# Attention on one core: small transfers of the row sums moved to the sync engine, with later steps for the reciprocal, the output and the stack loads

## The chip, the cores and the metric

The kernel runs on one core of one Trainium2 chip. The metric is device time in microseconds (us). Engines are named as in the profile: PE is TensorE (PEld its weight loads), DVE is VectorE, ACT is ScalarE, POOL is GpSimd, SP is the sync engine, which here only issues DMAs. "SPq" and "ACTq" in a row mean the sequencer of that engine, issuing a DMA.

## What is computed

A transformer block with modulation by a condition vector, in float32, for 4 sequences of 1024 tokens, width 512, 16 heads of 32:

```python
ada = jax.nn.silu(c) @ Wada.T + bada
shift_msa, scale_msa, gate_msa, shift_mlp, scale_mlp, gate_mlp = jnp.split(ada, 6, axis=-1)
h = modulate(rmsnorm(x, g1, D), scale_msa, shift_msa)
qkv = h @ Wqkv.T + bqkv          # reshaped to q, k, v of 16 heads
q = rmsnorm(q, gq, hd) * hd ** (-0.5)
k = rmsnorm(k, gk, hd)
attn = jax.nn.softmax(jnp.einsum('bhqd,bhkd->bhqk', q, k), axis=-1)
o = jnp.einsum('bhqk,bhkd->bhqd', attn, v)
...
x = x + gate_msa[:, None, :] * (o @ Wproj.T + bproj)
h = modulate(rmsnorm(x, g2, D), scale_mlp, shift_mlp)
x = x + gate_mlp[:, None, :] * (gelu(h @ Wfc1.T + bfc1) @ Wfc2.T + bfc2)
```

## The kernel before, in words

Three parts follow each other: a setup, attention (`build_attention`), and the projection with the MLP (`build_mlp`). The change lies in attention alone.

Attention is a sequence of 256 **steps** L. A step takes one tile of 128 keys against one chunk of 512 queries, for four heads at once. Eight steps (`NT`) make a **half**: all keys against one query chunk; this document numbers the steps in a half 0 to 7. Two halves make a **group** of four heads (`STEPS` = 16), four groups a sequence (`BSTEPS` = 64). Each half has a number `hh`, 0 to 31.

In a step TensorE multiplies scores (`qk`, line 431) in two pairs of heads, each into its own PSUM tile; ACT takes their exponential into one of three probability buffers (`exponentials`, line 591; `RING` = 3); one step later TensorE multiplies the probabilities with the values (`weigh`, line 444), and VectorE adds them up over the half (`add`, line 677: seven additions of 2.3 us per half). Exponentials wait until the buffer's old contents were both weighed and added. Scores of a step wait for the exponentials of the step before.

Between these, a plan made of tables fills TensorE's time with the projections for later groups. `FILL` gives 4 or 6 products of `unit_products` (line 496) or `v_products` (line 509) to a step. A finished "unit" (one 128 x 512 block of keys or queries of a group) goes through `raw_out` (708), `square` (572), `sum_squares` (468), `logarithm` (562), `inverse_root` (566) and `make_parts` (757 to 765, step table `FIN_AT`). SP stores its two parts to DRAM (`store_parts`, 359, 512 KB) and loads them back in stacked form (`load_stack`, 381, four DMAs of 256 KB per unit). The table `STACK_LOAD` says at which step SP does so: for keys of a group at the earliest in steps 1 (first half of the keys) and 2 of the group before; for queries of half 0 in step 1 of the second half of the group before, for queries of half 1 in step 1 of the group itself. Keys of half 1 are needed at step 4 of the group, queries at the start of their half.

At the end of a half its row sums are inverted. For half `hh`, in steps counted from the start of the next half (`ROWS, COMPACT, INVERT, INVERTED, SPREAD, OUT = 1, 2, 4, 4, 5, 7`):

- step 1: TensorE sums over partitions (`row_sums`, 461, waits for the half's last addition, which VectorE makes in step 0), ACT copies the result (`move_rows`, 598, waits for the output of the half before) and ACT issues its store to DRAM (600, 8 KB);
- step 2: ACT waits for the store's landing and issues the load in compact form, 128 x 16 (604);
- step 4: VectorE inverts the compact tile (`invert`, 697); ACT waits for it and issues the store of the inverse (608);
- step 5: ACT waits for that landing and issues four DMAs that spread the inverse over partitions (613, 64 KB each);
- step 7: VectorE waits for the spread and multiplies the output (`output`, 693); SP stores it (386). The PSUM bank of the output is wanted again by `weigh` in step 1 of the half after.

Each engine works its instructions in the order written: the loop over L in its block, with the table look-ups in the order in which they stand there. SP's loop has no wait of its own for a step; it runs ahead until one of its DMAs has to wait for a semaphore.

Of the kernel before, what the change touches and what calls it, by code (L numbers as in the profile page):

```python
# [22 lines left out]
P = 128  # L23
B, T, D = 4, 1024, 512
H, DH = 16, 32
FF = 4 * D
KT = D // P
HG = P // DH
NG = H // HG
CH = 512  # L30
NH = T // CH
NT = T // P
CT = CH // P
NC = B * NH
# [65 lines left out]
ROWS, COMPACT, INVERT, INVERTED, SPREAD, OUT = 1, 2, 4, 4, 5, 7  # L100
# [7 lines left out]
OUT_AT[AFTER] = NC * NG - 1  # L108
# [18 lines left out]
for step, n in FIN_AT.items():  # L127
    b, g, kind, half = UNIT[n]
    first = STEPS * (NG * b + g - 1)
    at = first + 1 + half if kind == "k" else first + NT * (half + 1) + 1  # L130
    STACK_LOAD.setdefault(max(step + 1, at), []).append(n)
# [141 lines left out]
def build_attention(nc, small, dram, wq_hi, wq_lo):  # L273
# [4 lines left out]
    with ExitStack() as ctx:  # L278
# [65 lines left out]
        def _(sp):  # L344
# [42 lines left out]

            load_x(0)
# [4 lines left out]
            for L in range(START, AFTER + 1):  # L393
# [161 lines left out]
        def _(act):  # L555
# [38 lines left out]
            def move_rows(hh):  # L594
# [4 lines left out]
                act.wait_ge(rows_moved, hh + 1)  # L599
                act.dma_start(dram["rows"], inverse[0:P:DH, :]).then_inc(rows_stored, 16)  # L600

            def load_compact(hh):
                act.wait_ge(rows_stored, 16 * (hh + 1))
                act.dma_start(compact[:], dram["rows"].rearrange("h (r n) -> (h r) n", n=SEEN)).then_inc(compact_in, 16)

            def store_inverse(hh):
                act.wait_ge(inverted, hh + 1)
                act.dma_start(dram["inverse"].rearrange("h (r n) -> (h r) n", n=SEEN), compact[:]).then_inc(inverse_stored, 16)

            def spread_inverse(hh):  # L610
                act.wait_ge(inverse_stored, 16 * (hh + 1))
                for h in range(HG):
                    act.dma_start(inverse[h * DH:(h + 1) * DH, :], dram["inverse"][h:h + 1, :].broadcast_to([DH, CH])).then_inc(inverse_in, 16)

            for L in range(START, AFTER):
# [17 lines left out]
                if L in COMPACT_AT:  # L633
                    load_compact(COMPACT_AT[L])
                if L in INVERTED_AT:
                    store_inverse(INVERTED_AT[L])
                if L in SPREAD_AT:
                    spread_inverse(SPREAD_AT[L])
# [24 lines left out]
        def _(dve):  # L663
# [103 lines left out]
            for L in range(START, AFTER):  # L767
# [22 lines left out]
                if L == ADA_MADE:  # L790
                    dve.wait_ge(ada_mm, 1)
                    dve.wait_ge(ada_bias_in, 16 * NA_LATER)
                    for r in ada_rows:
                        nc.vector.tensor_tensor(o_out[r, :], scores[0][r, 0, :], inverse[r, :], ALU.add).then_inc(ada_made, 1)
            add(AFTER - 1)
            output(NC * NG - 1)
# [582 lines left out]
```

## Time and profile before

| | us |
|---|---|
| median of 3 runs | 1949.16 (1948.32 to 1950.94) |
| the profiled execution, its own time | 1943.82 |
| its span in the trace | 1942.0 |
| attention, first scores product to last weighted product | 93.2 to 1083.0 |
| PE busy | 1782.4 (92%) |
| DVE busy | 1099.0 (57%) |
| ACT busy | 918.7 (47%) |
| POOL busy | 355.3 (18%) |

The profile is one execution; its own time stands beside its span, and the median beside both since other executions took some us longer. A window row gives, for a stretch, its length and the busy time of PE, PEld, DVE, ACT and POOL, then the granted clock of PE (1.00 is 2.4 GHz, 0.50 is 1.2 GHz), the busy share of the 16 DMA engines and GB/s. The stretches begin where the first scores product of a half begins. "DMA to landing" is the time from issue to the last byte's semaphore, as minimum, median and maximum over the DMAs asked for.

### The profile page before, as it was taken

The page shows a single profiled execution, that of the slowest core. Times are in us where ns is not written, and L with a number is a line of the kernel's source. Part 1 is how long each engine was busy: PE and PEld are TensorE (multiplying, and loading weights), DVE is VectorE, ACT ScalarE, POOL GpSimd, SP SyncE. Part 2 cuts the span into 40 slices and gives each one's busy share as a digit, 9 for nine tenths or more (in the row PEclk, how much of TensorE's full clock was granted, in tenths as well). Part 3 has the DMA queues.
Part 4 walks back from the last instruction along what each step waited for, and adds up shares of the span by engine and source line. Part 5 has one row for each costly group of instructions (what it writes and reads, how often), then busy time and mean ns, then how long its engine had stood idle before and what let it go on. Part 6 is the DMA issues. An engine that isn't in the chain of part 4 may idle for free. (4 is left out here: it accounts for less than half of the span.)

```text
span 1942.0 us, 23267 instructions
## 1 busy us (share of the span) xinstructions
PE 1782.4 (92%) x8368; PEld 1149.3 (59%) x8368; DVE 1099.0 (57%) x1343; ACT 918.7 (47%) x1110; POOL 355.3 (18%) x296
## 2 busy tenths in 40 slices
PE   3898998998999899998889579999999999999998
PEld 1554454444454444444323268787878787878787
DVE  4578788777878787866678665414232323233211
ACT  2276676666676667766668443222222222222221
POOL 1101000000000001000000232424232333333341
PEclk8999999999999999999989789999999999999999
DMA  5564544546543555354543423101111010102000
GB/s 193 141 170 129 141 122 111 139 107 153 131 115 100 136 142 127 90 127 119 133 110 72 136 87 103 50 28 49 27 49 27 32 38 21 55 6 70 5 28 22
DMA packets 137611, 176.69 MB, mean 91 GB/s; under 512 B 33668, under 2 KB 58244, under 8 KB 137528
## 3 DMA queue, kind: packets, MB, share of 16 engines
q1 hardware_dynamic: 107344, 149.89, 29.3%
q10 hardware_dynamic: 30184, 25.71, 4.6%
q8 instruction: 50, 0.82, 0.2%
q14 instruction: 33, 0.27, 0.0%
HBM read 124.63 MB, written 50.92 MB: 90 GB/s over the span
## 5 line engine op out<-in xcount | busy, mean ns | idle before, releaser
L591 ACT ACTIVATE probs<-scores,shift 128x1024 f32<-128x1024 f32 x512 | 548.2, 1113 | 208.9 <-PE scores L431 188.3
L677 DVE TENSOR_TENSOR sums<-sums,probs 128x2048 f32<-128x2048 f32 x192 | 442.2, 2303 | 39.0 <-ACT probs L591 35.1
L431 PE MATMUL scores<-q_stack,k_stack 128*128 128x512 f32 x1024 | 353.2, 431 | 29.7 <-ACT probs L591 29.7
L431 PEld LDWEIGHTS scores<-q_stack,k_stack 128*128 128x128 f32 x1024 | 174.8, 193 | 282.6 <-ACT probs L591 155.1
L1143 PE MATMUL acc<-w_hi,act_parts 128*128 128x512 f32 x1024 | 317.4, 391 | 0.0
L444 PE MATMUL pv<-probs,v 128*32 128x512 f32 x2048 | 278.3, 616 | 0.3 <-ACT probs L591 0.3
L1106 POOL TENSOR_TENSOR act_parts<-act_full,act_parts 128x512 fp32r<-128x512 f32 x128 | 169.7, 1326 | 499.5 <-ACT act_parts L1057 498.9
L1050 ACT ACTIVATE act_full<-up,f_bias 128x512 f32<-128x512 f32 x128 | 88.2, 689 | 336.3 <-PE up L1160 315.9
L1143 PEld LDWEIGHTS acc<-w_hi,act_parts 128*128 128x128 f32 x1024 | 190.7, 188 | 38.6
L1160 PE MATMUL up<-z_hi,w_hi 128*128 128x512 f32 x512 | 201.2, 393 | 5.1 <-POOL z_lo L1093 5.1
L1160 PE MATMUL up<-z_lo,w_hi 128*128 128x512 f32 x512 | 200.3, 391 | 0.0
L1160 PE MATMUL up<-z_hi,w_lo 128*128 128x512 f32 x512 | 200.2, 391 | 0.0
L1143 PE MATMUL acc<-w_lo,act_parts 128*128 128x512 f32 x512 | 199.4, 389 | 0.0
L1218 DVE TENSOR_TENSOR y_next<-proj,p_bias 128x512 f32<-128x512 f32 x28 | 19.3, 690 | 297.1 <-PE proj L1121 297.1
L1057 ACT ACTIVATE act_parts<-act_full 128x512 fp32r<-128x512 f32 x128 | 80.9, 632 | 222.5 <-PE acc L1143 221.4
L496 PE MATMUL gemm<-h_hi,wqkv_hi 128*128 128x512 f32 x256 | 104.7, 409 | 17.9 <-issue 14.9
L654 POOL TENSOR_TENSOR x_inv<-x_sqc,minus_half 128x1 f32<-128x1 f32 x32 | 17.6, 551 | 529.7 <-DVE x_sqc L729 529.7
L1160 PEld LDWEIGHTS up<-z_hi,w_hi 128*128 128x128 f32 x512 | 96.8, 189 | 25.4 <-POOL z_lo L1093 5.5
L444 PEld LDWEIGHTS pv<-probs,v 128*32 128x32 f32 x2048 | 41.4, 109 | 116.8 <-ACT probs L591 64.0
L1160 PEld LDWEIGHTS up<-z_hi,w_lo 128*128 128x128 f32 x512 | 96.8, 189 | 20.3
L1160 PEld LDWEIGHTS up<-z_lo,w_hi 128*128 128x128 f32 x512 | 96.8, 189 | 20.0
L1143 PEld LDWEIGHTS acc<-w_lo,act_parts 128*128 128x128 f32 x512 | 96.1, 188 | 20.2
(134 smaller groups left out, 2098.8 us busy)
## 6 DMA issues: line engine op xcount, KB each, us to landing
parts_scratch<-parts SPq DMA_DIRECT2D x64, 512.0 KB, 3.1
k_stack<-parts_scratch SPq DMA_DIRECT2D x128, 256.0 KB, 5.9
q_stack<-parts_scratch SPq DMA_DIRECT2D x128, 256.0 KB, 5.9
xt<-in_x SPq DMA_DIRECT2D x32, 256.0 KB, 3.6
heads_out<-o_out SPq DMA_DIRECT2D x32, 256.0 KB, 2.0
out<-result SPq DMA_DIRECT2D x32, 256.0 KB, 2.0
inverse<-inverse_scratch ACTq DMA_DIRECT2D x124, 64.0 KB, 2.0
heads<-heads_out SPq DMA_DIRECT2D x30, 256.0 KB, 3.5
```

Of the source, the lines that this page charges most:

```text
L431: mm = nc.tensor.matmul(scores[p][:, i, :], k_stack[s][:, h, j * P:(j + 1) * P], q_stack[half][:, h, :], start=True, stop=True)
L444: mm = nc.tensor.matmul(pv[hh % NH][h * DH:(h + 1) * DH, :], v[b % 2][:, j, (g * HG + h) * DH:(g * HG + h + 1) * DH], probs[l % RING][:, h ...
L496: mm = nc.tensor.matmul(gemm[:], w[:, k, at:at + P], h[:, k, c], start=(n == 0), stop=(n == len(terms) - 1))
L591: nc.scalar.activation(probs[L % RING][:, 2 * p:2 * p + 2, :], scores[p][:], ACT.Exp, bias=small["shift"][:]).then_inc(exp_done, 1)
L654: nc.gpsimd.tensor_tensor(x_inv[:, t:t + 1], x_sqc[:, t:t + 1], small["minus_half"][:, 0:1], ALU.pow).then_inc(inv_done, 1)
L677: nc.vector.tensor_tensor(sums[:], a[:], probs[l % RING][:], ALU.add).then_inc(added, 1)
L1050: nc.scalar.activation(act_full[m % 2][:], up[m % 2][:], ACT.Gelu_apprx_tanh, bias=f1_bias[:, m:m + 1]).then_inc(gelu_done, 1)
L1057: nc.scalar.activation(act_parts[m % 2][:, 0, :], act_full[m % 2][:], ACT.Copy).then_inc(act_hi, 1)
L1106: nc.gpsimd.tensor_tensor(act_parts[m % 2][:, 1, :], act_full[m % 2][:], full(act_parts[m % 2][:, 0, :]), ALU.subtract).then_inc(act_lo, 1)
L1143: mm = nc.tensor.matmul(acc[t][:], act_parts[m % 2][:, b, t * P:(t + 1) * P], w2[a][:, m, :], start=(m == 0 and i == 0), stop=(m == NM - 1 ...
L1160: mm = nc.tensor.matmul(up[m % 2][:], w1[a][:, k, m * P:(m + 1) * P], z[b][:, k, :], start=(k == 0 and i == 0), stop=(k == KT - 1 and i == 2))
L1218: nc.vector.tensor_tensor(yt, proj[:], p_bias[:], ALU.add).then_inc(proj_moved, 1)
```

## The change

The four kinds of small transfers are issued by SP instead of ACT. In SP's loop they stand at the head of a step, before the loads of x, the store of the output, the store of parts and the stack loads. The reciprocal with its store moves from step 4 to 5, the spread from 5 to 6, the output from 7 to 8 (which is step 0 of the half after), and one more turn of SP's loop and an `output` on VectorE are added at the end for the shift. Stack loads begin three steps later at the earliest: keys in steps 4 and 5, queries in step 4. For units that get ready later than that, nothing changes.

```diff
-ROWS, COMPACT, INVERT, INVERTED, SPREAD, OUT = 1, 2, 4, 4, 5, 7
+ROWS, COMPACT, INVERT, INVERTED, SPREAD, OUT = 1, 2, 5, 5, 6, 8
...
-OUT_AT[AFTER] = NC * NG - 1
+OUT_AT[AFTER + 1] = NC * NG - 1
...
     first = STEPS * (NG * b + g - 1)
-    at = first + 1 + half if kind == "k" else first + NT * (half + 1) + 1
+    at = first + 4 + half if kind == "k" else first + NT * (half + 1) + 4
...
+            def store_rows(hh):
+                sp.wait_ge(rows_moved, hh + 1)
+                sp.dma_start(dram["rows"], inverse[0:P:DH, :]).then_inc(rows_stored, 16)
+
+            def load_compact(hh):
+                sp.wait_ge(rows_stored, 16 * (hh + 1))
+                sp.dma_start(compact[:], dram["rows"].rearrange("h (r n) -> (h r) n", n=SEEN)).then_inc(compact_in, 16)
+
+            def store_inverse(hh):
+                sp.wait_ge(inverted, hh + 1)
+                sp.dma_start(dram["inverse"].rearrange("h (r n) -> (h r) n", n=SEEN), compact[:]).then_inc(inverse_stored, 16)
+
+            def spread_inverse(hh):
+                sp.wait_ge(inverse_stored, 16 * (hh + 1))
+                for h in range(HG):
+                    sp.dma_start(inverse[h * DH:(h + 1) * DH, :], dram["inverse"][h:h + 1, :].broadcast_to([DH, CH])).then_inc(inverse_in, 16)
...
-            for L in range(START, AFTER + 1):
+            for L in range(START, AFTER + 2):
+                if L in ROWS_AT:
+                    store_rows(ROWS_AT[L])
+                if L in COMPACT_AT:
+                    load_compact(COMPACT_AT[L])
+                if L in INVERTED_AT:
+                    store_inverse(INVERTED_AT[L])
+                if L in SPREAD_AT:
+                    spread_inverse(SPREAD_AT[L])
...
                 nc.scalar.activation(inverse[:], aux[:], ACT.Copy).then_inc(rows_moved, 1)
-                act.wait_ge(rows_moved, hh + 1)
-                act.dma_start(dram["rows"], inverse[0:P:DH, :]).then_inc(rows_stored, 16)
...
-                if L in COMPACT_AT:
-                    load_compact(COMPACT_AT[L])
-                if L in INVERTED_AT:
-                    store_inverse(INVERTED_AT[L])
-                if L in SPREAD_AT:
-                    spread_inverse(SPREAD_AT[L])
...
+            output(OUT_AT[AFTER])
             add(AFTER - 1)
-            output(NC * NG - 1)
+            output(OUT_AT[AFTER + 1])
```

**First order:** SP in the first half from step 128, before. The rows are the parts store of step 128, a load of x and the stack loads of steps 129 and 130 (keys, queries, keys), the parts store of step 133, the output of step 135 and the parts store of step 136.

```order
L359 DMA parts_scratch<-parts 128x2x512 [waits part_lo]
L349 DMA xt<-in_x 128x512 [waits turned]
L381 DMA k_stack<-parts_scratch 32x4x512 [waits qk_mm,parts_stored]
L381 DMA k_stack<-parts_scratch 32x4x512 x3
L381 DMA q_stack<-parts_scratch 32x4x512 [waits qk_mm,parts_stored]
L381 DMA q_stack<-parts_scratch 32x4x512 x3
L381 DMA k_stack<-parts_scratch 32x4x512 [waits qk_mm,parts_stored]
L381 DMA k_stack<-parts_scratch 32x4x512 x3
L359 DMA parts_scratch<-parts 128x2x512 [waits part_lo]
L386 DMA heads_out<-o_out 128x512 [waits o_done]
L359 DMA parts_scratch<-parts 128x2x512 [waits part_lo]
```

**Second order:** the same stretch of SP with the change, from the compact load of step 130 on (the row sums' store, 390, and the load of x stand ahead of it).

```order
L394 DMA compact<-rows_scratch 128x16 [waits rows_stored]
L381 DMA k_stack<-parts_scratch 32x4x512 [waits qk_mm,parts_stored]
L381 DMA k_stack<-parts_scratch 32x4x512 x3
L381 DMA q_stack<-parts_scratch 32x4x512 [waits qk_mm,parts_stored]
L381 DMA q_stack<-parts_scratch 32x4x512 x3
L398 DMA inverse_scratch<-compact 128x16 [waits inverted]
L359 DMA parts_scratch<-parts 128x2x512 [waits part_lo]
L381 DMA k_stack<-parts_scratch 32x4x512 [waits qk_mm,parts_stored]
L381 DMA k_stack<-parts_scratch 32x4x512 x3
L403 DMA inverse<-inverse_scratch 32x512 [waits inverse_stored]
L403 DMA inverse<-inverse_scratch 32x512 x3
L386 DMA heads_out<-o_out 128x512 [waits o_done]
```

The four small transfers are SP's now. The compact load stands ahead of all stack loads, the store of the inverse (398) behind eight of them, and the spread (403) behind four more and a parts store.

**Third order:** SP with the change in the half from step 208, where no projections are left.

```order
L390 DMA rows_scratch<-inverse 4x512 [waits rows_moved]
L394 DMA compact<-rows_scratch 128x16 [waits rows_stored]
L359 DMA parts_scratch<-parts 128x2x512 [waits part_lo]
L381 DMA k_stack<-parts_scratch 32x4x512 [waits qk_mm,parts_stored]
L381 DMA k_stack<-parts_scratch 32x4x512 x3
L381 DMA q_stack<-parts_scratch 32x4x512 [waits qk_mm,parts_stored]
L381 DMA q_stack<-parts_scratch 32x4x512 x3
L398 DMA inverse_scratch<-compact 128x16 [waits inverted]
L381 DMA k_stack<-parts_scratch 32x4x512 [waits qk_mm,parts_stored]
L381 DMA k_stack<-parts_scratch 32x4x512 x3
L403 DMA inverse<-inverse_scratch 32x512 [waits inverse_stored]
```

Here the parts store of step 212 stands between the compact load and the stack loads, so these wait for VectorE's `make_parts`. The twelve loads that stood in steps 209 and 210 before are on both sides of the inverse's store.

**Fourth order:** VectorE at the end of a half, around step 136; before, and below it with the change (lines 677, 693, 718 and 757 of before are 681, 697, 722 and 761 there).

```order
L677 TENSOR_TENSOR sums<-sums,probs 128x2048 [waits added,exp_done]
L718 TENSOR_TENSOR v<-gemm,v_bias 128x512 [waits pv_mm,v_mm]
L693 TENSOR_TENSOR o_out<-pv,inverse 128x512 [waits o_stored,pv_mm,inverse_in]
L677 TENSOR_TENSOR sums<-sums,probs 128x2048 [waits added,exp_done] x2
L757 SCALAR_TENSOR_TENSOR raw<-norms,raw 128x512 [waits norm_done]
L763 TENSOR_SCALAR parts<-raw 128x512 [waits parts_stored,normed]
```

```order
L681 TENSOR_TENSOR sums<-sums,probs 128x2048 [waits added,exp_done]
L722 TENSOR_TENSOR v<-gemm,v_bias 128x512 [waits pv_mm,v_mm]
L681 TENSOR_TENSOR sums<-sums,probs 128x2048 [waits added,exp_done]
L697 TENSOR_TENSOR o_out<-pv,inverse 128x512 [waits o_stored,pv_mm,inverse_in]
L681 TENSOR_TENSOR sums<-sums,probs 128x2048 [waits added,exp_done]
L761 SCALAR_TENSOR_TENSOR raw<-norms,raw 128x512 [waits norm_done]
```

The output product moved behind one addition: it stood ahead of the half's last two, and now stands directly ahead of the last, behind which the parts of step 136 are made (757 before, 761 now).

## Rows read from the trace of the kernel before

**Rows 1.** The page, part 1: busy us (share) xinstructions.

```profile
PE 1782.4 (92%) x8368; PEld 1149.3 (59%) x8368; DVE 1099.0 (57%) x1343; ACT 918.7 (47%) x1110; POOL 355.3 (18%) x296
```

**Rows 2.** Windows over nine first halves, steps 64 to 207; columns: stretch, us, busy (instructions).

```profile
625.34:661.95 36.61, 30.89 (x153) 15.71 (x149) 24.54 (x27) 21.62 (x25) 1.85 (x2) 0.91 0.58 137
...
sum 315.83, PE 276.94 PEld 141.43 DVE 223.09 ACT 197.19 POOL 12.95; mean PE 30.77 PEld 15.71 DVE 24.79 ACT 21.91 POOL 1.44
```

**Rows 3.** Windows over the nine second halves of the same groups.

```profile
661.95:690.18 28.23, 27.93 (x148) 13.89 (x144) 24.82 (x26) 21.26 (x25) 2.85 (x2) 1.00 0.37 104
...
sum 256.49, PE 254.45 PEld 129.79 DVE 212.95 ACT 189.88 POOL 22.03; mean PE 28.27 PEld 14.42 DVE 23.66 ACT 21.10 POOL 2.45
```

**Rows 4.** Waits, whole program: who for whom, us, times, longest.

```profile
DVE compact L697 <- DMA compact<-rows_scratch: 85.3, 20, 8.8
```

**Rows 5.** Timeline of PE, 640 to 654 us; columns: start, us, engine, line.

```profile
641.57 0.40 PE L496 MATMUL gemm<-h_hi,wqkv_lo 128*128 128x512 f32 x1
641.81 0.40 PE L496 MATMUL gemm<-h_hi,wqkv_hi 128*128 128x512 f32 x1
...
649.76 0.77 PE L509 MATMUL gemm<-wqkv_hi,h_hi 128*128 128x512 f32 x1 [4.97 <-issue]
650.32 0.63 PE L509 MATMUL gemm<-wqkv_lo,h_hi 128*128 128x512 f32 x1
```

**Rows 6.** Timeline of SP, 628 to 648 us.

```profile
630.41 2.25 SPq L381 DMA_DIRECT2D k_stack<-parts_scratch  x4
...
634.94 1.80 SPq L381 DMA_DIRECT2D k_stack<-parts_scratch  x4
```

**Rows 7.** Timeline of ACT, 631 to 654 us.

```profile
631.24 0.60 ACT L598 ACTIVATE inverse<-aux 128x512 f32<-128x512 f32 x1
631.87 0.51 ACTq L600 DMA_DIRECT2D rows_scratch<-inverse  x1
...
637.83 0.34 ACTq L604 DMA_DIRECT2D compact<-rows_scratch  x1
```

**Rows 8.** Timeline of DVE, 640 to 655 us.

```profile
646.60 0.25 DVE L697 RECIPROCAL compact<-compact 128x16 f32<-128x16 f32 x1 [7.82 <-DMA compact<-rows_scratch]
```

**Rows 9.** Line 604 alone at 637.8 us.

```profile
DMA to landing us min/median/max: 8.7/8.7/8.7
```

**Rows 10.** Line 604 alone at 1049.4 us.

```profile
DMA to landing us min/median/max: 1.5/1.5/1.5
```

**Rows 11.** Line 381, 630.4 to 636.4 us.

```profile
DMA to landing us min/median/max: 4.8/8.9/13.5
```

**Rows 12.** Lines 608 and 613, whole program.

```profile
DMA to landing us min/median/max: 1.4/1.4/4.5
DMA to landing us min/median/max: 1.9/2.0/3.5
```

**Rows 13.** Line 349 alone at 166.0 us, issued behind eight stack loads.

```profile
DMA to landing us min/median/max: 9.2/9.2/9.2
```

**Rows 14.** Timeline of DVE and of PE, 660 to 669 us.

```profile
661.91 2.29 DVE L677 TENSOR_TENSOR sums<-sums,probs 128x2048 f32<-128x2048 f32 x1 [1.26 <-ACT probs L591]
...
666.57 1.07 PE L461 MATMUL aux<-sums,ones 128*32 128x512 f32 x8
```

**Rows 15.** Groups by line, 30 to 1200 us: sum-of-squares products; output product.

```profile
L468 PE MATMUL aux<-squares,head_ones 128*128 128x512 f32 x128 | 65.7, 594 | 3.7 <-ACT squares L572 3.7
...
L693 DVE TENSOR_TENSOR o_out<-pv,inverse 128x512 f32<-128x512 f32 x32 | 21.9, 683 | 0.0
```

**Rows 16.** Windows over four halves from step 208 on.

```profile
944.18:972.41 28.23, 22.39 (x110) 7.99 (x107) 16.69 (x13) 18.87 (x21) 0.00 (x0) 0.88 0.67 160
...
995.84:1022.19 26.35, 20.89 (x109) 7.17 (x105) 16.60 (x10) 17.04 (x18) 0.00 (x0) 0.87 0.64 140
...
1042.07:1061.80 19.73, 18.94 (x109) 6.45 (x105) 16.67 (x10) 17.35 (x18) 0.00 (x0) 1.00 0.36 82
```

**Rows 17.** Windows over the eight halves before step 64.

```profile
sum 278.66, PE 257.55 PEld 136.24 DVE 223.07 ACT 189.42 POOL 19.08; mean PE 32.19 PEld 17.03 DVE 27.88 ACT 23.68 POOL 2.38
```

More of the change, by code:

```diff
@@ L598, in move_rows @@
                 nc.scalar.activation(inverse[:], aux[:], ACT.Copy).then_inc(rows_moved, 1)
-                act.wait_ge(rows_moved, hh + 1)
-                act.dma_start(dram["rows"], inverse[0:P:DH, :]).then_inc(rows_stored, 16)
[L602 to L613, printed above, removed]
             for L in range(START, AFTER):
```

## The prediction

> **What bounds the kernel now.** I read the page's busy times first. TensorE is busy 92% of the 1942 us span, the next engine 57% [rows 1]. So only what makes TensorE wait, or run at its lower clock, can be saved. The change touches attention alone, 256 steps between 93 and 1083 us. I then cut attention into halves of eight steps (a "half" has one query chunk for four heads; two make a group) and compared windows. Over steps 64 to 207 the nine first halves of a group last 315.83 us together, the nine second halves 256.49 [rows 2, 3]. In the second halves TensorE is busy for 254.45 us of that, at granted clock 1.00; a first half like 625.34 to 661.95 has clock 0.91. Both kinds do nearly the same work. By the plan the first halves have 328 projection products against 320, at about 0.24 us each by their starts [rows 5], and 20 sums of squares against 16, at 65.7 / 64 = 1.03 us [rows 15], at most. That is 1.9 + 4.1, say 5.5 us as neighbouring products overlap. Of the difference of 59.3 us about 54 us is waiting, and 2 us more sits in the second halves (256.49 - 254.45). So **56 us** are lost here.
>
> The timelines of one first half, the one that starts at 625.34, say to what. At 630.4 SP issues twelve stack loads of 256 KB in a row [rows 6]. They land 4.8 us after issue for the first and 13.5 us for the last, issued 5.9 us later [rows 11]: one each (13.5 + 5.9 - 4.8) / 11 = 1.33 us. ACT moves the row sums at 631.24 and issues their 8 KB transfer at 631.87; the next transfer, which waits for its landing, is issued only at 637.83 [rows 7]. It takes 8.7 us [rows 9], where the same transfer with nothing beside it takes 1.5 [rows 10]. VectorE stands in its queue before the small reciprocal for 7.82 us [rows 8]; over the program such waits sum to 85.3 us in 20 places [rows 4]. Additions queue behind it, the ring of three probability buffers fills, ACT stops, and TensorE idles 4.97 us. Its next products are 0.56 us apart by their starts (649.76, 650.32) where they were 0.24 [rows 5]: they run at 1.2 GHz, the lower of its two levels, instead of 2.4.
>
> **The change, part by part.** Times are from the start of a first half, with steps as in the windows.
>
> Row sums and compact load. Moved at +5.9 and done at +6.5 as before. The transfer is now SP's, and the stack loads that stood ahead of it are in step 4 or later. SP is not paced by steps, only by its waits, so they follow the compact load at once. I take 1.7 us for the row sums (bounds: 1.5 as the compact load alone, 6.0 as now, 631.87 to 637.83) because nothing large is ahead; the compact load is issued at +8.3 and lands at about +10. The reciprocal, one step later, stands at about +18 (five eighths of a 28.5 us half). **The wait of 7.8 us and the two waits on ACT go**, and with them the clock loss. That is the term of -56 us.
>
> ACT loses seven DMA issues per half, some 3 us by the 0.51 and 0.34 us of two of them [rows 7]. ACT is busy 197 of 316 us in these halves [rows 2], and its idle time covers them; 0 us. If TensorE's cover were gone they would be worth up to 3 us a half.
>
> Stack loads. Eight of them (keys of the next group, queries of the second half) are issued from +8.7; the eighth lands at 8.7 + 4.8 + 7 x 1.33 = +22.8. The queries are wanted at step 8, about +28.5. Margin 5.7 us: 0 us.
>
> Inverse store and spread. The store stands at +18.2 with loads outstanding until +22.8. A tile load issued behind eight stack loads took 9.2 us [rows 13], so I let SP's transfers land in order: store at +24 (1.4 us alone, [rows 12]). The last four key loads were issued meanwhile and land until 22.8 + 5.3 = +28.1. The spread is issued at +24 and lands behind them, with 1.9 to 2.0 us of its own, at **+30**. Who waits: VectorE's output, ahead of the half's last addition, then the row sums on TensorE. At the half that ends at 661.90 that addition started at 661.91 after 1.26 us idle, and the row sums at 666.57 [rows 14], 4.67 after the half's end. So the spread may land until 28.5 + 4.67 - 2.29 - 0.68 (output product, [rows 15]) = +30.2 at no cost. Just hidden. In the four first halves from steps 80, 128, 144 and 192 a 512 KB parts store stands ahead of the key loads (the second order below shows it), two loads' worth, 2.7 us: the spread lands at about +32.8, 2.6 us late. With the clock after it I take 3 us for each, **+12 us** (bounds 0 and 5 us each: the present stall of 5 with its low clock).
>
> The output step. The output moves from ahead of the seventh addition to ahead of the eighth; the 0.68 us lie in the 1.26 us that VectorE idles there [rows 14]. 0 us; without that cover 31 x 0.68 = 21 us.
>
> Halves without projections, from step 208. They last 19.73 us when nothing disturbs [rows 16], so the same transfers have less room. Half 208: a parts store of step 212 stands ahead of the loads (third order below). I put it at +15.3 (four steps of 2.5, an addition, 2 us of parts), so the eighth load lands at 15.8 + 4.8 + 9.3 = +30. The half takes 30 instead of 28.23. Its spread lands behind four more loads, at +37, and the row sums wait until +40 instead of +34.7: +5 us, against 3.5 us (23.43 - 19.9 by the rule of the undisturbed half) that the next half loses now. Half 224: 5.6 + 1.7 + 0.3 puts the eighth load at +22, so it takes 22 instead of 26.35, but the spread lands at +29.5 and costs 6. Together 1.8 + 5.3 - 3.5 - 4.3 + 5.8 = **+5 us** (bounds -13, when both become 20 us, and +20).
>
> Halves before step 64. 278.66 us with 257.55 busy [rows 17], 21 us idle. Compact waits are few there; most idleness is VectorE's own chain of parts, and new waits behind loads arise. I take **-5 us**, bounds -15 and +8.
>
> The Trainium skill, "DMA: Bandwidth & Descriptors", section "Queues, rings and completion order", says that a DMA engine takes turns by packets between the rows of SP and ACT. By that rule a small transfer on ACT's row overtakes SP's backlog, and the change gives that up: left on ACT's row the spread would land some 4 us sooner, and the 12 us of late spreads would not arise (sum -56). The trace agrees little: on ACT's row the compact load still took 8.7 us [rows 9], about as long as a load of SP's behind the backlog [rows 13].
>
> Sum: -56 + 12 + 0 + 5 - 5 = **-44 us**. The profiled execution took 1943.8 us; it would become 1899.8. The median of the runs shown is 1949.2, 5.4 higher, and I set the forecast against that: **1905 us**.
>
> **The rivals.**
>
> (a) The stall is handed on: the small transfers land, but store and spread wait longer behind the loads than I let them. For it: the slack is 0.2 us on paper. Against it: the loads' pace is a measured one. With 2 us more in each of the 14 halves that have eight or more loads, 28 us of the 44 go: 1933 us, and 1924 to 1939 for 1.3 to 2.5 us more.
>
> (b) Slower than before. One mechanism: the order on SP's queue puts the spread behind twelve loads, and SP itself waits for the inverse store before it issues the next parts store. The present stalls sum to about 76 us (56, 10 from step 208 on, 10 before step 64) over 14 halves, 5.4 each. The new one is as long once the twelfth load lands 5.6 us later, which is at 1.33 + 5.6 / 12 = 1.80 us a load; from there on this case decides. At 1.95 us a load each half loses 7.2 us, 101 in all instead of 76: 1949 + 25 = 1974 us. The rule of that page of the Trainium skill leans this way, since by it only ACT's row gives a small transfer a path around the loads. Against it: 1.33 us were measured with loads and small transfers together.
>
> (c) Nothing is gained: the waits are TensorE's for something else, and the reciprocal's wait is cover. For it: VectorE idles in other places too. Against it: the second halves, with four loads instead of twelve and the same rest, have none of the loss. 1945 to 1953 us.
>
> (d) All goes: neither the four late spreads nor the halves from 208 on cost anything, and the early halves gain 15. -56 - 13 - 15 puts it at 1865; more likely 1875 to 1887.
>
> **How the numbers follow.** Forecast case 0.70, from 1888 to 1924 (the bounds of the three uncertain terms, not all at one end). Rival (a) 0.12, (b) 0.08, (c) 0.04, (d) 0.06. The range 1887 to 1932 us holds the forecast case and about half of (a) and little of the others, some 0.8. A difference within 0.2%, 3.9 us, is about what a measurement of this kernel can't tell from none. Faster by more: 0.70 + 0.12 + 0.06 = 0.88. Same 0.04 (c). Slower 0.08 (b).
>
> **What would show it.** Right: VectorE's waits for the compact load fall from 85 us to under 10, row sums and compact load take under 3 us each, the nine first halves last about 270 us instead of 316, their clock is at 0.97 or more. New and expected: VectorE's output product waits for the inverse's spread in the halves from 80, 128, 144, 192, 208 and 224. Wrong: the output's wait shows in most first halves with 3 us or more, or scores products wait for query stacks at step 8 of filled halves; then (a) or (b) holds. If the waits for the compact load are gone and the first halves last 310 us, it is (c).

## The result, and the profile after

The changed kernel takes **1893.9 us** (median of 4 runs, 1893.5 to 1894.7) against 1950.1 us of the kernel before on the same chip: ratio 0.9713, 95% interval 0.9697 to 0.9728. The forecast was 1905, range 1887 to 1932: right in sign, 11 us too high. The profiled span fell from 1942.0 to 1892.3 us. TensorE's busy time fell with it, though it does the same work [rows 1]; the page of the changed kernel, part 1:

```profile
PE 1767.5 (93%) x8368; PEld 1141.6 (60%) x8368; DVE 1101.9 (58%) x1343; ACT 920.6 (49%) x1110; POOL 364.7 (19%) x296
```

The windows of the changed kernel, cut at the same steps. First its nine first halves, with the one that answers to 625.34 [rows 2], then the nine second halves [rows 3], the eight halves before step 64 [rows 17], and those from step 208 on [rows 16]:

```profile
603.06:631.66 28.60, 28.60 (x152) 14.73 (x148) 24.00 (x25) 21.63 (x25) 2.86 (x2) 1.00 0.67 159
...
sum 260.75, PE 259.29 PEld 133.04 DVE 220.23 ACT 197.29 POOL 20.10; mean PE 28.81 PEld 14.78 DVE 24.47 ACT 21.92 POOL 2.23
...
sum 255.73, PE 254.06 PEld 129.92 DVE 218.46 ACT 190.81 POOL 23.08; mean PE 28.23 PEld 14.44 DVE 24.27 ACT 21.20 POOL 2.56
...
267.14:305.94 38.80, 34.19 (x156) 17.14 (x156) 25.08 (x29) 24.03 (x27) 3.36 (x3) 0.91 0.46 120
...
sum 279.20, PE 260.40 PEld 136.75 DVE 222.62 ACT 189.71 POOL 20.27; mean PE 32.55 PEld 17.09 DVE 27.83 ACT 23.71 POOL 2.53
...
889.04:919.71 30.67, 19.93 (x111) 6.95 (x107) 19.99 (x15) 19.34 (x21) 0.00 (x0) 0.92 0.55 134
919.71:945.11 25.40, 22.63 (x105) 7.98 (x105) 15.92 (x9) 17.14 (x17) 0.00 (x0) 0.83 0.39 89
945.11:964.70 19.59, 18.92 (x109) 6.36 (x105) 16.66 (x10) 17.46 (x18) 0.00 (x0) 1.00 0.63 138
964.70:990.57 25.87, 20.27 (x108) 6.52 (x104) 16.74 (x10) 17.56 (x18) 0.00 (x0) 0.93 0.46 101
...
sum 142.25, PE 120.72 PEld 40.71 DVE 104.16 ACT 106.80 POOL 0.00; mean PE 20.12 PEld 6.78 DVE 17.36 ACT 17.80 POOL 0.00
```

All of the gain is in the first halves, 315.83 to 260.75 us: the half at 603.06 has TensorE busy throughout at clock 1.00, where its counterpart took 36.61 us at 0.91. The second halves gain 0.8 us, the early halves lose 0.5, those from 208 on lose 3.5 (142.25 against 138.78), and the rest of the program is 2.1 us longer. Together -49.7 us of span.

Waits of the changed kernel, whole program (who for whom, us, times, longest). The 85.3 us for the compact load [rows 4] have no successor under that name; the output waits instead:

```profile
DVE o_out L697 <- DMA inverse<-inverse_scratch: 36.7, 9, 12.8
...
PE scores L456 <- DMA q_stack<-parts_scratch: 10.2, 2, 9.8
```

The half from 603.06 in the timeline of SP (start, us, engine, line, operation, tiles), then DVE's and PE's rows of the same stretch:

```profile
609.59 0.50 SPq L390 DMA_DIRECT2D rows_scratch<-inverse  x1
...
611.26 0.32 SPq L394 DMA_DIRECT2D compact<-rows_scratch  x1
611.68 1.80 SPq L381 DMA_DIRECT2D k_stack<-parts_scratch  x4
613.58 1.80 SPq L381 DMA_DIRECT2D q_stack<-parts_scratch  x4
620.84 0.34 SPq L398 DMA_DIRECT2D inverse_scratch<-compact  x1
624.97 0.38 SPq L359 DMA_DIRECT2D parts_scratch<-parts  x1
625.45 2.30 SPq L381 DMA_DIRECT2D k_stack<-parts_scratch  x4
627.80 1.83 SPq L403 DMA_DIRECT2D inverse<-inverse_scratch  x4
```

```profile
620.57 0.24 DVE L701 RECIPROCAL compact<-compact 128x16 f32<-128x16 f32 x1
...
634.31 0.69 DVE L697 TENSOR_TENSOR o_out<-pv,inverse 128x512 f32<-128x512 f32 x1 [4.37 <-DMA inverse<-inverse_scratch]
...
637.26 1.06 PE L486 MATMUL aux<-sums,ones 128*32 128x512 f32 x8 [0.90 <-DVE sums L681]
```

From issue to landing in this half: line 394 at 611.3, line 381 from 611.5, line 398 at 620.8, line 403 from 627:

```profile
DMA to landing us min/median/max: 2.5/2.5/2.5
DMA to landing us min/median/max: 3.4/6.1/8.6
DMA to landing us min/median/max: 4.0/4.0/4.0
DMA to landing us min/median/max: 5.1/5.4/5.8
```

The compact load is now issued ahead of the stack loads and lands in 2.5 us instead of 8.7 [rows 9]; the reciprocal finds its operand there; the inverse's store lands 4.0 us after its issue, 1.3 us behind the last of the eight loads; then a parts store and four more loads go ahead of the spread, which lands at 634.3. VectorE's output waits 4.37 us, and TensorE loses 0.90.

Six of the nine waits of the output lie where the prediction had put them, in the halves from 80, 128, 144, 192, 208 and 224 (1.4, 4.4, 1.3, 4.2, 12.8 and 4.9 us); three were not forecast (6.0 us in the half from step 32, 1.1 and 0.6). One sign of being right was not met in full: the compact load takes 1.5 to 6.1 us, over 3 in 7 of 31 cases.

### The profile page after: what moved, and what is told of

It is laid out like the page before. It is cut to its first block and busy times, and to the rows that moved or that the text cites. A ratio compares the mean times of both kernels' runs of the same rounds, so it can differ in the third digit from the quotient of the medians.

```text
span 1892.3 us, 23267 instructions
## 1 busy us (share of the span) xinstructions
PE 1767.5 (93%) x8368; PEld 1141.6 (60%) x8368; DVE 1101.9 (58%) x1343; ACT 920.6 (49%) x1110; POOL 364.7 (19%) x296
## 5 line engine op out<-in xcount | busy, mean ns | idle before, releaser
L681 DVE TENSOR_TENSOR sums<-sums,probs 128x2048 f32<-128x2048 f32 x192 | 444.9, 2317 | 42.6 <-ACT probs L616 38.4
L456 PE MATMUL scores<-q_stack,k_stack 128*128 128x512 f32 x1024 | 348.2, 426 | 16.6 <-DMA q_stack<-parts_scratch 10.2
```

Of the source, the lines that this page charges most:

```text
L456: mm = nc.tensor.matmul(scores[p][:, i, :], k_stack[s][:, h, j * P:(j + 1) * P], q_stack[half][:, h, :], start=True, stop=True)
L681: nc.vector.tensor_tensor(sums[:], a[:], probs[l % RING][:], ALU.add).then_inc(added, 1)
```

## The experiments

Three parts can be put in alone: the stack loads three steps later (**loads**), the issues on SP (**sync**), and reciprocal, store, spread and output one step later (**steps**). Measured beside the first four kernels below, the kernel before took 1949.9 us.

### Each part by itself

```diff
# loads
-    at = first + 1 + half if kind == "k" else first + NT * (half + 1) + 1
+    at = first + 4 + half if kind == "k" else first + NT * (half + 1) + 4
# steps
-ROWS, COMPACT, INVERT, INVERTED, SPREAD, OUT = 1, 2, 4, 4, 5, 7
+ROWS, COMPACT, INVERT, INVERTED, SPREAD, OUT = 1, 2, 5, 5, 6, 8
...
```

```diff
# sync: the four functions leave ACT's program for SP's, called first in each step
+                if L in ROWS_AT:
+                    store_rows(ROWS_AT[L])
+                if L in COMPACT_AT:
+                    load_compact(COMPACT_AT[L])
...
```

Loads alone, on the kernel before:

> The kernel before with one edit: the stack loads begin three steps later; ACT still issues the four small transfers, reciprocal, spread and output at the old steps. Loads theory (the gain is the stack loads standing behind the row sums' store and the compact load): 1895 to 1910 us, VectorE's waits for the compact load under 15 us in sum, first halves from step 64 at about 262 us. Sync theory (the gain is ACT freed of issues and of waits for landings): 1940 to 1950. Steps theory (the gain is the reciprocal one step later): 1940 to 1950.

Sync alone:

> The changed kernel with old steps and old stack loads: only the issuing engine changes. Loads theory: the compact load now stands behind eight stack loads on SP's queue and lands at about +20 to +23 us of a half, so the reciprocal waits as long as before or longer: 1945 to 1980 us. Sync theory: 1895 to 1910.

Steps alone:

> The kernel before with reciprocal and its store, spread and output one step later, nothing else. Loads theory: the compact load lands as late as before (8 to 9 us), the wait before the reciprocal shortens by at most one step of 3 to 4 us, from about 6 to about 3; TensorE's stall and its time at 1.2 GHz shrink with it: 1915 to 1935 us. Steps theory: 1895 to 1910. If the waits on ACT alone matter: 1940 to 1950.

Loads and steps, with ACT's issues:

> The changed kernel with only the issuing engine undone: ACT issues the small transfers. Loads theory: ACT's issues lie in its idle time, so 1888 to 1900 us, no more than 6 us from the changed kernel; the spread is on ACT's row and need not land behind the stack loads, so the output's waits of 37 us in sum should nearly vanish if the rows take turns, and stay if they do not. Sync theory: 1935 to 1950.

Measured, with the sum of the nine first halves, and VectorE's waits for the compact load:

| kernel | us | ratio (95%) | first halves | compact waits |
|---|---|---|---|---|
| before | 1949.9 | 1 | 315.8 | 85.3 in 20 |
| loads | 1934.9 | 0.9928 (0.9901 to 0.9955) | 307.5 | 62.8 in 17 |
| sync | 1991.4 | 1.0221 (1.0198 to 1.0244) | 332.3 | 133.3 in 29 |
| steps | 1900.1 | 0.9755 (0.9725 to 0.9785) | 277.4 | 28.7 in 11 |
| loads, steps | 1905.3 | 0.9771 (0.9753 to 0.9788) | 271.1 | 20.6 in 8 |
| all (the change) | 1893.9 | 0.9713 (0.9697 to 0.9728) | 260.7 | none |

The times are medians; the two columns on the right are of one profiled execution each.

With the loads alone I had expected most of the gain, since they would no longer stand ahead of the compact load. They still do. By the tables 56 of the 64 units are loaded later in SP's program, but SP is not paced by steps: later in its program is later in time only where something that waits stands between. In the loads-only kernel's half from 561.59 nothing does. Eight loads follow the parts store of step 113 as in the kernel before, from 567.71 (+6.1 both times), and ACT issues the compact load behind them. Only in the first halves from 80, 128, 144 and 192, where a parts store stands between the old place and the new, do four of the twelve loads move, from about +10 to +25. Timelines of SP and of ACT in the half from 561.59, and the compact load's landing:

```profile
567.24 0.37 SPq L359 DMA_DIRECT2D parts_scratch<-parts  x1
567.71 2.29 SPq L381 DMA_DIRECT2D q_stack<-parts_scratch  x4
570.09 1.80 SPq L381 DMA_DIRECT2D k_stack<-parts_scratch  x4
```

```profile
572.03 0.34 ACTq L604 DMA_DIRECT2D compact<-rows_scratch  x1
```

```profile
DMA to landing us min/median/max: 8.6/8.6/8.6
```

Sync alone makes it worse. In the first halves the compact load is issued with seven or eight stack loads outstanding on SP's own row, in the second halves with four, and the reciprocal still stands at step 4, so its waits rise to 133.3 us. What the steps bring is another thing: with them alone the compact load lands as late as before (+18.9 to +21.3 in the first halves), but the reciprocal, at +16 to +19, waits 1.6 to 4.0 us and not 5.0 to 8.4. That alone takes 38.4 of the 55.1 us that the change takes out of the first halves.

One pair was not run: loads and sync with the old steps. So it is not shown how much the change would gain without the later steps.

### Order or engine

With sync on top of loads and steps, 11.4 us go. Two theories: ORDER, that SP's program places the compact load ahead of the stack loads, and ENGINE, that ACT comes late to its issues and loses time by them. The compact load moved behind the stack loads of its own step:

```diff
# SP's loop of the changed kernel
-                if L in COMPACT_AT:
-                    load_compact(COMPACT_AT[L])
...
                 for n in STACK_LOAD.get(L, ()):
                     load_stack(n)
+                if L in COMPACT_AT:
+                    load_compact(COMPACT_AT[L])
```

> The changed kernel, with one difference: in a step of SP the compact load stands behind the stack loads of that step instead of ahead of them. Theory ORDER (a small transfer lands once everything issued before it on either row has landed, and not sooner): the compact load lands at about +20 to +22 of a first half instead of +10 to +12, VectorE waits for it again (50 to 90 us in all), the nine first halves last 280 to 300 us instead of 261, the kernel takes 1915 to 1935 us. Theory ENGINE (what pays is that SP issues, since ACT comes late to its issues and loses time by them): SP still issues all, so the time stays at 1893 to 1898 us.

1893.8 us, ratio 0.9707 (0.9691 to 0.9723). This decided nothing: in the step of the compact load there are hardly any stack loads, they stand in later steps, and from step 96 on there was still no stack load outstanding at any compact load. It serves as a second measurement of the change, beside the next three kernels.

ACT issues all four, and SP waits for the compact load's landing before it goes on:

```diff
# on the kernel with loads and steps
+                if L in COMPACT_AT:
+                    sp.wait_ge(compact_in, 16 * (COMPACT_AT[L] + 1))
```

> Loads and steps as in the changed kernel, all four small transfers issued by ACT as before, and SP made to wait, before it issues anything of the step of the compact load, until ACT's compact load has landed. Theory ORDER: no stack load is ahead of the compact load, which is issued at about +10.4 and lands at +12, so VectorE's waits for it fall from 20.6 us to under 3, the first halves last 261 to 265 us, the kernel takes 1892 to 1899 us; the loads start 3 us later than in the changed kernel, which may cost up to 3 us more in the halves from 208. Theory ENGINE: ACT's seven issues and its waits for landings stay, so the time stays at 1902 to 1908 us, as with these issues on ACT without the gate (1905.3).

1903.5 us, 0.9752 (0.9736 to 0.9769): the waits for the compact load are gone, as ORDER says, and the time stays, as ENGINE says. Its first halves take 273.1 us, and 10.4 of the 12.4 us above the change's are in two of them, 33.64 and 33.89 us. Window of the first, and ACT's timeline in it:

```profile
487.41:521.05 33.64, 30.65 (x152) 14.90 (x148) 26.98 (x27) 21.56 (x24) 3.21 (x2) 0.93 0.64 161
```

```profile
506.80 0.34 ACTq L610 DMA_DIRECT2D inverse_scratch<-compact  x1
...
514.64 1.76 ACTq L615 DMA_DIRECT2D inverse<-inverse_scratch  x4
516.50 0.63 ACT L574 ACTIVATE squares<-raw 128x512 f32<-128x512 f32 x1 [5.32 <-issue]
```

ACT must wait for the store's landing, 7.8 us behind the stack loads, before it may issue the spread, and exponentials stand in its row behind that. Six of the other seven first halves last as long as the change's within 0.1 us, with the seven issues on ACT. So the issues themselves cost nothing, as I had said. The **landings that an issue waits for** are a candidate, and I had not priced them. But the order of the loads changed too. In the change SP's row holds the last four key loads of such a half behind the inverse's store, which they follow at 505.69; with the store on ACT nothing holds them, and twelve loads go in a row. SP's rows for these four loads, of this kernel and, below it, of the change:

```profile
502.90 2.07 SPq L381 DMA_DIRECT2D k_stack<-parts_scratch  x4
```

```profile
505.69 1.80 SPq L381 DMA_DIRECT2D k_stack<-parts_scratch  x4
```

The store then takes 7.8 us instead of 6.4, and since ACT issues it 2.8 us later in the half (+19.4 against +16.6) it lands at +27.2 instead of +23.0. The halves that are longer, from 96 and 160 and by 2.1 us that from 64 (31.70 against 29.59), are just the three in which all twelve loads go ahead of the store; in the other six four of them stand behind a parts store, or come later, in both kernels. What a blocked ACT costs by itself and what the late store costs is not separated.

Rows and compact load on SP, store and spread on ACT:

```diff
# the functions as in the kernel before, called from ACT's loop, in the changed kernel
+                if L in INVERTED_AT:
+                    store_inverse(INVERTED_AT[L])
+                if L in SPREAD_AT:
+                    spread_inverse(SPREAD_AT[L])
```

> The changed kernel with row sums and compact load issued by SP, but the inverse's store and its four spread transfers issued by ACT. Theory ORDER: the store lands behind the loads issued before it whichever engine issues it, so 1892 to 1898 us and VectorE's output waits stay at 25 to 40 us. Theory ENGINE: ACT gets five of its seven issues back and reaches them late, 1899 to 1904 us. Theory TURNS (the rows of SP and ACT are served in turn by packets): store and spread overtake SP's loads, output waits fall under 10 us, 1884 to 1890 us.

1897.6 us, 0.9726 (0.9710 to 0.9742): 4 us above the second measurement of the change (1893.8), with intervals that overlap. The first halves took 268.6 us (the same three stand out, 31.5, 31.9 and 31.2, again with twelve loads ahead of the store), the early ones 274.4, 5 less. The output's waits stayed at 37.1 us in 11 places, and in those three halves the store took 6.6 to 7.9 us with six loads outstanding and landed 0.2 to 0.5 us after the last of them. So TURNS falls for the store: on ACT's row it does not overtake them.

Sync and steps, the loads in their old steps (the changed kernel with the line of the loads put back):

> The changed kernel with the stack loads begun in the old steps: SP issues and the later steps alone. Theory ORDER: eight loads stand ahead of the compact load in a first half, it lands at +20 to +22 and the reciprocal at +18 waits 2 to 5 us; VectorE's waits for it 30 to 60 us, first halves 275 to 295 us, kernel 1905 to 1925 us: later than with ACT's issues (1900.1), since the parts store and the input load are also ahead. Theory ENGINE: 1900.1 less some 11 us, 1886 to 1892 us.

1927.0 us, 0.9878 (0.9861 to 0.9895): 27 us slower than the steps with ACT's issues (1900.1, measured beside other runs; 24 us by the ratios), just beyond what ORDER gave and far from ENGINE. Timeline of SP in its half from 623.54, and the landings of the eight loads (line 381 from 631) and of the compact load (line 394 at 635.0):

```profile
633.04 1.95 SPq L381 DMA_DIRECT2D q_stack<-parts_scratch  x4
635.03 0.43 SPq L394 DMA_DIRECT2D compact<-rows_scratch  x1
```

```profile
DMA to landing us min/median/max: 4.0/6.7/9.4
DMA to landing us min/median/max: 9.1/9.1/9.1
```

Eight loads ahead, 9.1 us; in this kernel with four ahead 5.0 to 6.2; at the end, with none, 1.5. So the moved loads are worth 33 us once SP issues (1927.0 to 1893.9), 15 us by themselves, and on top of the steps alone nothing that can be told (1900.1 and 1905.3, with intervals that overlap). The parts' values don't add.

### The output's step

The changed kernel with the output back at step 7:

```diff
-ROWS, COMPACT, INVERT, INVERTED, SPREAD, OUT = 1, 2, 5, 5, 6, 8
+ROWS, COMPACT, INVERT, INVERTED, SPREAD, OUT = 1, 2, 5, 5, 6, 7
...
```

> The changed kernel with the output back at step 7, the reciprocal, its store and the spread at their later steps. The spread lands at +24 to +31 of a half and the output stands at +21 to +25, ahead of the seventh addition: VectorE waits 1 to 7 us in most first halves, over 80 us in all instead of 36.7; first halves 275 to 295 us instead of 261, kernel 1910 to 1930 us. If the output's step is of no account, 1892 to 1896 us.

1948.6 us, 0.9986 (0.9973 to 0.9998): the whole gain is gone, and the time is 18 us above what I expected at most. There are no waits for the compact load, and the first halves keep their gain (264.2 us); the second halves take 283.9 us instead of 255.7, and the output's waits rise to 83.8 us in 22 places. Timelines of VectorE and of TensorE at the end of the half from 443.45:

```profile
477.25 0.69 DVE L697 TENSOR_TENSOR o_out<-pv,inverse 128x512 f32<-128x512 f32 x1 [4.48 <-DMA inverse<-inverse_scratch]
477.86 2.28 DVE L681 TENSOR_TENSOR sums<-sums,probs 128x2048 f32<-128x2048 f32 x1
480.06 0.68 DVE L722 TENSOR_TENSOR v<-gemm,v_bias 128x512 f32<-128x512 f32 x1
```

```profile
480.79 0.62 PE L521 MATMUL gemm<-h_hi,wqkv_hi 128*128 128x512 f32 x1 [4.47 <-DVE v L722]
481.22 0.63 PE L521 MATMUL gemm<-h_lo,wqkv_hi 128*128 128x512 f32 x1
```

A wait of 4.48 us in VectorE's row stops TensorE for 4.47, since the move of v, which frees a projection bank, stands behind it; the products after it are 0.43 us apart instead of 0.24, and the clock of the half that begins at 475.59 is 0.95. In the change the move of v goes ahead of this output (459.44), which waits 1.45 us for its spread, and TensorE does not stop:

```profile
461.57 0.69 DVE L697 TENSOR_TENSOR o_out<-pv,inverse 128x512 f32<-128x512 f32 x1 [1.45 <-DMA inverse<-inverse_scratch]
```

Even its wait of 4.37 us, at the end of the half from 603.06, costs TensorE only 0.90, and the clock stays at 1.00.

And the output alone one step later, on the kernel before:

```diff
-ROWS, COMPACT, INVERT, INVERTED, SPREAD, OUT = 1, 2, 4, 4, 5, 7
+ROWS, COMPACT, INVERT, INVERTED, SPREAD, OUT = 1, 2, 4, 4, 5, 8
...
```

> The kernel before with the output alone one step later; reciprocal, store and spread stay where they were, as do the loads and ACT's issues. Theory PLACE OF THE WAIT (what stalls TensorE is how early in VectorE's row the waiting reciprocal stands; the output's step only has to stay behind the spread): the waits for the compact load stay at 80 to 90 us and the time at 1945 to 1952 us. Theory SLACK (one step more between the late reciprocal and the output is what lets the later work through, since the output in its old step costs 55 us in the changed kernel): the first halves lose some 10 to 20 of their 316 us, 1925 to 1940 us.

1952.3 us, 1.0004 (0.9989 to 1.0020), with its waits for the compact load:

```profile
DVE compact L697 <- DMA compact<-rows_scratch: 86.6, 21, 8.6
```

PLACE OF THE WAIT holds. The output's step brings nothing by itself, and without it the rest of the change, the later reciprocal included, brings nothing either.

### A version that beats both

The changed kernel still issues key loads between store and spread. Here all keys of a group go behind the spread, and in the first of the two kernels the queries one step earlier:

```diff
-    at = first + 4 + half if kind == "k" else first + NT * (half + 1) + 4
+    at = first + 7 if kind == "k" else first + NT * (half + 1) + 3
```

> The changed kernel with the eight key stack loads of a group begun at its step 7, behind the spread, and the query stack loads at step 3 of a half, ahead of a parts store of step 4. Theory SPREAD (the late spreads and the half at 267 us, with its 38.8 us, come from loads and parts stores between the inverse's store and its spread): VectorE's output waits fall from 36.7 us to under 15, the halves before step 64 together last some 272 us instead of 279, and half 208 takes 28 us instead of 30.7 as its queries no longer wait for a parts store: 1880 to 1888 us. Theory FREE (these waits are hidden, as the first halves' 260.75 us with 259.29 of TensorE say): the first and second halves stay within 1 us and only the tail gains, 1889 to 1893 us. If the keys now push something else late (row sums behind eight key loads in the second half), output waits move there and it takes 1895 or more.

> As the kernel with keys at step 7 and queries at step 3, but the queries left at step 4. The difference of the two is what the queries' step is worth: half 208 stays at 30 to 31 us, the steps from 208 on at 141 to 143 us, so 2 to 5 us slower than the other. Against the changed kernel it shows the keys alone: 1884 to 1890 us under SPREAD, 1892 to 1895 us under FREE.

**1864.1 us**, 0.9549 (0.9532 to 0.9565), and 1869.2 us, 0.9580 (0.9561 to 0.9600), with the queries at step 4. Both are faster than either theory gave. Windows of the first kernel, second halves, halves before 64 and from 208 on, and its waits:

```profile
sum 253.76, PE 253.76 PEld 130.08 DVE 216.45 ACT 190.61 POOL 21.69; mean PE 28.20 PEld 14.45 DVE 24.05 ACT 21.18 POOL 2.41
...
sum 267.57, PE 254.10 PEld 134.54 DVE 222.50 ACT 189.60 POOL 20.29; mean PE 31.76 PEld 16.82 DVE 27.81 ACT 23.70 POOL 2.54
...
875.34:896.12 20.78, 19.85 (x111) 6.94 (x107) 17.95 (x15) 19.03 (x21) 0.00 (x0) 1.00 0.40 116
...
sum 125.67, PE 118.31 PEld 39.78 DVE 104.16 ACT 106.81 POOL 0.00; mean PE 19.72 PEld 6.63 DVE 17.36 ACT 17.80 POOL 0.00
```

```profile
DVE o_out L697 <- DMA inverse<-inverse_scratch: 1.5, 2, 1.3
```

The output's waits fall from 36.7 to 1.5 us. Steps 64 to 207 gain only 2.0 us, all in the second halves, close to what FREE says. The early halves gain 11.6 us, 7.7 of it in the half from 267.14 (38.80 to 31.10), in which the output waited 5.97 us for the spread. Those from 208 on gain 16.6 us: 9.9 in half 208 (30.67 to 20.78), where TensorE had stood 9.81 us for the query stacks and not for a spread, and 6.3 in the half from step 232 (25.87 to 19.60), in which an output had waited 4.9 us for its spread. The queries' step is 5.1 us of the whole gain.

## Why the prediction was right, and where not

**What bounds the kernel** held. The 56 us of waiting in steps 64 to 207 were there to be had: these steps are 55.8 us shorter, and in the first halves TensorE now idles 1.46 us in 260.75.

**The -56 us came about as written down.** SP runs ahead, the compact load stands ahead of the loads in its program, and in the half from 603.06 the row sums take 1.7 us to the next issue (forecast 1.7), the compact load lands at +10.7 (+10), the loads start at +8.6 (+8.7; +5.1 before the change) and the eighth lands at +20.5 (+22.8). What I left out is that the later reciprocal, which I gave no value of its own, does most of it alone: 38.4 us of the first halves' 55.1, with the compact load landing as late as ever. The early landing brings the other 16.7 there. In the kernel as a whole it leaves only 6 us (1900.1 to 1893.9), since the halves before 64 and from 208 on are 3.7 and 5.5 us longer than with the steps alone. And my first expectation for the loads alone, 1895 to 1910 us against 1934.9, forgot what the prediction says, that SP is not paced by steps.

**ACT's issues, 0 us:** with them on ACT instead of SP the kernel is 11.4 us slower. The issues themselves were rightly free. What came with the move was not: the compact load's place behind the loads (20.6 us of waits there), and the inverse's store, which goes out later on ACT and behind more loads.

**The late spreads, +12 us, were mis-sized.** The store was put at +24 and landed at +21.8 (4.0 us after 620.84); the spread was put at +32.8 and landed at +31.2 (634.3 in the half from 603.06), 1.6 us earlier. The slack was read right: TensorE lost 0.90 us. But I took 3 us for each of four, with the clock behind it, and after so short a stop the clock stayed at 1.00. All late spreads of steps 64 to 207 cost at most 2.0 us, by the best version, which hasn't them: 10 us less than the term. A small slip in the slack: the half ended at 661.95, not 661.90, which is 0.05 us.

**The output's step, 0 us,** is right for the move (nothing by itself), but I named no price for its absence beyond 21 us. It is 55.

**Halves from 208, +5 us:** measured +3.5, and near the forecast half by half. Half 208 30.67 us (forecast 30), its spread lands at +35.6 (+37). Half 224 19.59 (22); the half after it 6.0 longer than before (5.8). Timeline of SP in half 208, and TensorE's wait at its end:

```profile
904.79 0.37 SPq L359 DMA_DIRECT2D parts_scratch<-parts  x1
...
919.94 1.71 SPq L403 DMA_DIRECT2D inverse<-inverse_scratch  x4
```

```profile
919.71 2.07 PE L456 MATMUL scores<-q_stack,k_stack 128*128 128x512 f32 x4 [9.81 <-DMA q_stack<-parts_scratch]
```

The parts store is at +15.8 (forecast +15.3), the queries behind it land at +30.6 (forecast +30).

**Halves before 64, -5 us:** measured +0.5. The bounds held. New waits behind loads, which I had named, took part of the gain: in the half from 267.14 the spread that the output waited for landed at 273.1, six us into the half.

**The sum.** Measured against the terms: -57.8 (forecast -56), +2.0 (+12), +3.5 (+5), +0.5 (-5), and +2.1 in the rest of the program, for which I have no cause and had no term. That is -49.7 us of span against -44. The other 5.4 us of the miss come from the level: the execution that the sum was made against stood 5.4 us under the median of its kernel, that of the changed kernel (1894.1) stands at its own.

**The rivals.** (a) did not come: outside the four forecast halves only one output of steps 64 to 207 waits, 0.6 us. (b) did not come: the eight loads of the half from 603.06 land from 615.1 to 623.6, 1.22 us each, far from 1.80. But its mechanism is real, since SP's issues with the old steps and loads gave 1991 us. (c) and (d) did not come; (d)'s early gain was open to a different edit.

## What to carry to other kernels

Where small transfers share the DMA engines with large ones, what counted in these runs was how many large ones were issued ahead, so let the program order, not a start time, decide: small load, then large loads, and no large one between a store and the load that waits for it. An issue that must wait for a landing is safer on an engine whose row holds nothing urgent; what it costs on a busy one was not measured alone. A wait is priced by what stands behind it in its engine's row: one of 4.5 us stopped TensorE for 4.5 with the clock on top, one of 4.4 us for 0.9 and left the clock. And parts of such a change can't be priced one by one: test them in pairs.

## What the runs showed of the hardware

The compact load (8 KB) on the two rows, over all kernels, by how many stack loads of 256 KB were outstanding at its issue. On SP's row with 7 or 8 of them it took 7.8 to 10.7 us, and landed 0.17 to 0.35 us after the last of them, in all 30 cases. On ACT's row with 7 or 8 it took 7.4 to 10.1 us. With 9 to 11, in 11 cases, it took 8.5 to 8.9 us all the same and landed 1.1 to 4.2 us **ahead** of the last load. One case, in the kernel with the steps alone: the compact load at 621.2, and the stack loads that were issued from 613 to 620, of which the last, issued at 619.56, took the 12.4 us:

```profile
DMA to landing us min/median/max: 8.7/8.7/8.7
DMA to landing us min/median/max: 4.8/8.7/12.4
```

It lands at 629.9, that load at 632.0. So a small transfer on ACT's row does overtake a part of the backlog, but only what is beyond some 8.5 us of it; of eight loads it waits out nearly all on either row (on ACT's row with 7 or 8 it landed from 1.3 us before to 0.7 us after the last of them). SP's row had no case with more than eight, so beyond that the rows can't be compared. What holds the first part in order is open. The Trainium skill, "DMA: Bandwidth & Descriptors", section "Queues, rings and completion order", says that a DMA engine takes turns between the rows by packets. By that rule alone I would not expect the compact load on ACT's row to take 8.7 us in the kernel before; the runs agree with it only for loads beyond the eighth.
